# The two later long attentions of a 12-stage Perceiver kernel: running maximum over chunks of 2, 3 and 2 supers in place of 3, 2 and 2

## What is computed

```python
q = (x @ Wq.T + bq)                      # 64 tokens, 16 heads of 8
k, v = ctx @ Wk.T + bk, ctx @ Wv.T + bv  # 6272 keys
att = softmax(q . k / sqrt(8), over the 6272 keys)
x = x + (att @ v) @ Wo.T + bo
```

## Time and profile before

| | us |
|---|---|
| median of 3 runs | 697.67 |
| lowest, highest of the 3 | 692.69, 701.86 |
| the profiled execution's own time | 696.98 |
| its span, first to last instruction | 695.0 |
| mean granted clock of PE over the span | 0.818 of 2.4 GHz |
| PE, DVE, ACT busy | 524.0, 435.9, 301.9 |
| long attention of level 1, its first instruction to the last maximum's user | 160.3 to about 278 |
| long attention of level 3 | 539.8 to 660.6 |

### The profile page before, as it was taken

How to read it: one execution, slowest core, us unless ns; L and a number is a source line. 1 busy time by engine, 2 the same in 40 slices (tenths; PEclk the granted TensorE clock), 3 DMA queues, 4 the chain that set the end, 5 groups by cost and what they waited for, 6 DMA issues and landing times. The chain is left out here.

```text
span 695.0 us, 11989 instructions
## 1 busy us (share of the span) xinstructions
PE 524.0 (75%) x4779; PEld 323.4 (47%) x4779; DVE 435.9 (63%) x837; ACT 301.9 (43%) x363; POOL 132.0 (19%) x197
## 2 busy tenths in 40 slices
PE   8799976878989998347900791945797788999847
PEld 5455653666345555213400371733355524555536
DVE  6642216755667775745999999754556566777143
ACT  2578861424847766111700640110222374776611
POOL 2110100000000000204698999001000000000000
PEclk9999996889589999656955696975559778999959
DMA  8333272352300000001000030002080270000000
GB/s 210 70 96 82 69 271 88 89 115 48 116 1 2 2 2 2 2 1 47 0 0 0 1 140 0 0 1 97 25 182 22 66 287 1 2 2 2 2 1 3
DMA packets 16766, 37.34 MB, mean 54 GB/s; under 512 B 5291, under 2 KB 14684, under 8 KB 15996
## 3 DMA queue, kind: packets, MB, share of 16 engines
q1 hardware_dynamic: 16648, 36.46, 18.4%
q0 software_dynamic: 64, 0.11, 0.1%
HBM read 21.90 MB, written 0.03 MB: 32 GB/s over the span
## 5 line engine op out<-in xcount | busy, mean ns | idle before, releaser
L249 POOL TENSOR_TENSOR rstd<-rstd,minus_half 64x1 f32<-64x1 f32 x20 | 11.7, 587 | 447.5 <-DVE rstd L257 447.5
L1394 ACT ACTIVATE ring<-psum,l3x_gain_columns 128x1024 f32<-128x1024 f32 x49 | 54.4, 1114 | 26.5 <-PE psum L1284 26.5
L1394 ACT ACTIVATE ring<-psum,l1x_gain_columns 128x1024 f32<-128x1024 f32 x49 | 54.4, 1114 | 25.4 <-PE psum L1284 25.3
L1298 PE MATMUL psum<-ring,values 128*32 128x128 f32 x1568 | 62.7, 279 | 0.4 <-ACT ring L1394 0.4
L843 ACT ACTIVATE ring<-psum,l0x_key_scale 128x1024 f32<-128x1024 f32 x49 | 52.5, 1114 | 13.4 <-PE psum L736 9.4
L1298 PEld LDWEIGHTS psum<-ring,values 128*32 128x32 f32 x1568 | 37.0, 109 | 24.8 <-issue 19.6
L1507 DVE TENSOR_REDUCE l3x_tops<-psum 128x1 f32<-128x448 f32 x64 | 36.3, 618 | 9.4 <-PE psum L1273 9.4
L1507 DVE TENSOR_REDUCE l1x_tops<-psum 128x1 f32<-128x448 f32 x64 | 36.3, 618 | 9.4 <-PE psum L1273 9.4
L3099 DVE MAX8 l2x_best<-values 128x8 f32<-128x6272 f32 x6 | 40.1, 6691 | 0.1
L3107 DVE MATCH_REPLACE8 values<-l2x_best,values 128x6272 f32<-128x6272 f32 x6 | 40.1, 6675 | 0.0
L2957 PE MATMUL psum<-ring,l2x_refuse 128*128 128x512 bf16 (+1 forms) x13 | 5.5, 422 | 40.5 <-ACT ring L3040 40.5
(11 more groups left out here) (777 smaller groups left out, 1106.6 us busy)
## 6 DMA issues: line engine op xcount, KB each, us to landing
experts<-in_experts SPq DMA_DIRECT2D x1, 4608.0 KB, 13.4
wide<-experts SPq DMA_DIRECT2D x82, 56.0 KB, 2.0
experts<-in_experts SPq DMA_DIRECT2D x1, 4096.0 KB, 14.9
wide<-experts SPq DMA_DIRECT2D x36, 112.0 KB
ring<-in_ctx_tiles SPq DMA_DIRECT2D x1, 2352.0 KB, 9.0
experts<-in_experts SPq DMA_DIRECT2D x1, 2048.0 KB, 7.8
ctx_t<-in_ctx_t SPq DMA_DIRECT2D x3, 672.0 KB, 7.8
wide<-ring SPq DMA_DIRECT2D x12, 168.0 KB
```

The costliest lines, as they stand in the source:

```text
L1298: last = nc.tensor.matmul(ps[32 * quarter:32 * quarter + 32, O_BANK, 128 * half:128 * half + 128], mem.values[:, at:at + 32], probs[:, t % ...
L1394: nc.scalar.activation(probs[:, t % PROBS, :].rearrange("p (b n) -> p b n", b=2), ps[:, pair:pair + 2, :], ACT.Exp, scale=exp_gain[:, :]). ...
```

## The change

`MAX_SUPERS` becomes `[2, 3, 2]`. Everything else follows from it:

```diff
-MAX_SUPERS = [3, 2, 2]
+MAX_SUPERS = [2, 3, 2]
```

## The result

The changed kernel takes 716.02 us (median of 4 runs, 715.31 to 718.13) against 696.50 (692.69 to 701.86, four runs, one more than in the table of the kernel before): a ratio of 1.028, 95% interval 1.021 to 1.035. It is slower by 19.5 us. The forecast was 703, with 696 to 713 as its range, and a chance of 10 in 100 for slower by over 2%. The profiled execution took 715.63 us, span 713.9, mean granted clock 0.794 (696.98, 695.0 and 0.818 before).

The account below looks back on a forecast made before the run. The front was taken as a chain with every round on the path, chunk 0 as PE-bound, chunk 1 as DVE-bound. 2 x 9.4 less 13.0 gave +5.9 us, forecast 703, range 696 to 713.

Parts of the forecast that it names:

- The removed round: Front of each attention: one full round of the chain goes, 6.69 us in level 1 and 6.30 in level 3.
- The added maxima at full clock: Chunk 0: 48 maxima at 0.557 us plus eight gaps of about 0.18, 28.2 us; loop +9.4 us in each attention.
- Chunk 1 at 23.8: Chunk 1: 32 maxima over 16 tiles at 1.50 us each take 23.8 us, where it was 18.73.
- the 6.45 between the chunks: From DVE's last maximum of a chunk to the next chunk's first: 6.45 us, taken as unchanged.
- the sum of +5.9: Whole kernel: 2 x 9.4 less 13.0 gives +5.9 us; likeliest case, rival A, 73 in 100.
- term (b): Turned maximum behind the front: an earlier or later clock rise could shift time by -2.4 to +2.4 us; nothing taken.
- the weighing of the clock: Chunk 0: judged by chunk 1's granted clock of 1.00, the clock would not fall, so the sum stands.
- rival B: Clock falls in chunk 0: 712 us with one attention hit, 722 with both; chance 10 in 100.
- Its price: Fallen clock in chunk 0: gaps of 1.4 in place of 0.18, eight of them adding 9 to 10 us an attention.
- The rule of the Trainium skill: Cycling through PSUM banks with brief idling swings the clock; by it chunk 0 would run partly at 1.2 GHz.
- Rival C: Outside the changed parts, the clock falls well: not slower, 692 to 697 us; chance 17 in 100.

Follow-up runs that it names:

- start_fill: Changed kernel plus ten matmuls whose result nobody reads, six while PE waits for the query stack, four for the first exponential: 702.21 us, ratio 1.003.
- fill_exps: Changed kernel plus only four matmuls nobody reads, before the wait for the first exponential: 705.3 us profiled; repeated ten times, median 701.58 us, ratio 1.005.
- level1_only: Chunks of 2, 3 and 2 in level 1's attention alone, level 3's left at 3, 2 and 2 as in the kernel before: 707.09 us, ratio 1.012.
- gentle_start: Changed kernel with chunk 0's 48 maxima dealt 2, 2, 6, 6, 6, 7, 6, 6, 7 over its nine tiles: 704.06 us, ratio 1.006.
- crowded_start: Kernel before (chunks of 3, 2 and 2) with chunk 1's 32 maxima dealt over chunk 0's first six tiles: 720.64 us, ratio 1.029.
- after_again: The changed kernel run once more, unaltered, against the kernel before: 714.93 us (median of 6), ratio 1.023.

## Why the prediction was wrong

*The removed round* was right: -6.67 and -6.38 where -6.69 and -6.30 stood.

*The added maxima at full clock* were right: with the clock up, start_fill, fill_exps and level1_only's level 1 span 57.6 us against 57.9 forecast, with gaps of 0.17 to 0.18 behind a first one of 0.38 (level1_only). Chunk 1 at 23.8 and the 6.45 between the chunks (6.47) held as well. So the sum of +5.9 describes the change without the clock, if a little too high. By the rows it is 2 x (57.6 - 48.4) = 18.4, less 13.05 for the rounds and 0.88 from the MEMSET to the first maximum (term (b), most of it in level 3), +4.5. The times agree: start_fill's 1.003 and fill_exps_again's 1.005 are 2 to 3 us, gentle_start's 1.006 is 4, and the upper ends of their intervals 5 to 7.

*The step that failed* is the weighing of the clock: "by the nearer row, chunk 1's 1.00, it would not, and the sum above stands." Chunk 1's row was near to chunk 0's middle, and of that it was right: gentle_start ran six and seven maxima a tile at 1.00. It said nothing of the loop's opening. There the kernel before had two maxima in tile 0, after which PE went straight on to `weigh` and the next `scores`; the changed kernel has five, of which two wait for a bank, behind two idle times of 1.27 and 0.86 us. In three of the four falls seen in it the clock went down 1.4 to 1.5 us after the first maximum, in tile 0; in the fourth it went 1.6 us ahead of it. The prediction names neither of the two idle times, which the kernel before has too, and so did not see that the new waits for banks would join them in one place. Where the second is filled (fill_exps_again) or the new waits come two tiles later (gentle_start), the clock holds. So rival B, given 10 in 100, was the outcome.

*Its price* was right a tile: gaps of 1.4 forecast, 1.41 measured. It was too high an attention, 9 to 10 us, because it let the clock stay down over all eight changes of tile. It came back after five, and the fall cost 63.7 - 57.6 = 6.1 us an attention, 12.2 in both. With the 4.5 above that makes the 16.7 of the table. The forecast's own 5.9 in its place would give 715.1 for the profiled execution, close to its 715.6 only because the stages outside gave 2 us more.

*The rule of the Trainium skill* ("TensorE: Matmul & The Clock Gate", section "A second HAM failure mode: psum-queue depth-cycling") named the outcome that came. As a cause it fits only in part. This case's trace agrees that a kernel which waits for PSUM banks between groups of matmuls can lose its clock; it does not agree that the cycling does it by itself, since the seven crowded tiles of gentle_start, and all nine of start_fill, kept it.

*Rival C* (clocks elsewhere) did not show: what lies outside the rows of the table differs by 2.2 us in all, and for the worse.

*What stays open.* In four of five profiled openings of this kind the clock fell, and in the fifth, with the same instructions and the same waits in the opening, it held. The table of openings points to the time since the clock's last rise, 4.2 us in three of the falls, 10.05 in the fourth and 5.07 where it held. No run moved that distance on purpose, so that it decides is not shown. How long the clock stayed down varied too, from 6.8 us (crowded_start, level 3) to 23.9 (after_again, level 3), and nothing here tells why.

## What to carry to other kernels

Look at a loop's opening by itself when a change makes PE wait there. Here idle times before the loop and new waits in its first tile came together in one place, and four matmuls that nobody reads, put right in front, kept 6 us an attention. When work for the next chunk is dealt over the tiles of this one, deal it evenly over all tiles before its due time, across chunks too, and compare each tile with the engine that would do it: a maximum more costs DVE's 0.557 us in a tile where DVE is the bound, and PE's 0.19 where PE is (1.50 us a tile with two, 1.12 with none).

## What the runs showed of the hardware

The busy share of PE in the profile does not tell which level of the clock a stretch will have. Once the clock had fallen PE had no idle time left, 19.48 of 19.48 us busy in the changed kernel and 15.00 of 15.00 in crowded_start, and the granted clock stayed at 0.50 all the same. Tiles of the same kind at the upper level, with PE busy only 7.42 of 9.12 us, kept 1.00. And whether it falls is not a property of the program alone: two executions with the same opening, its idle times of 1.27 and 0.86 us equal in both, went different ways.
